# Latent attention with a gated feed-forward: one row maximum over two spans, a low half on GpSimd, and new owners for small steps

## The chip, the cores and the metric

The kernel runs on one core of a Trainium2 chip. The metric is the device time of one execution in microseconds (us). A core has five engines that run side by side, each with its own queue of instructions: TensorE (PE), VectorE (DVE), ScalarE (ACT), GpSimd (POOL) and SyncE (SP), which here issues nearly all DMAs. They wait for one another through semaphores.

## The reference, cut to what matters

`x` is 1 x 2048 x 256. After a layer norm it goes through causal attention of 16 heads with latent keys (a 64 wide latent and a 64 wide rotated part) and, beside it, through a gated feed-forward; the results are multiplied and added to `x`.

```
q = (x @ wq); kva = x @ wkv_a
ckv = rmsnorm(kva[..., :64]) * kv_norm_scale;  k_pe = rope(kva[..., 64:])
scores = (q_nope . k_nope + rope(q_pe) . k_pe) * scale, causal
out = softmax(scores) @ v @ wo
g = silu(down(silu(gate(xn)) * up(xn)));  x = x + out * g
```

## The kernel before, in words

Heads go in 8 pairs, A and B. The weights are absorbed, so that each head scores a 128 wide query against one 128 x 2048 key tile. In float32 every product is split into a high and a low half: queries and keys into `_hi` and `_lo` (three matmuls for one product), probabilities into two float16 halves.

The attention is a pipeline of 128 units `u`, 16 to a pair. Unit `u` belongs to head `u % 2` and takes two tiles of 128 query rows: a big one, tile 15 - k, and a small one, tile k, with `k = step_of(u) = u % 16 // 2` from 0 to 7. Its keys come in three spans: span 0, keys 0 to 1023 of the big tile; span 1, the rest of the big tile, (8 - k) x 128 wide; span 2, the small tile, (k + 1) x 128 wide. So spans 1 and 2 together are always 1152 wide. The text below calls `u % 16` the step, 0 to 15. What a unit passes through:

- PE: `scores` of the spans into five PSUM banks (`s_ps`). Banks of span 1 directly follow those of span 0. A bank is written again only after the exponential of the unit before has read it.
- DVE: `row_max` (L922). One maximum over span 0, one over span 1 (both to `part_max`, L929), a small one over these two (L932), and one over span 2 (L927).
- ACT: `exponentials` (L789) of each span to `prob`, `prob_high` (L795, recorded on L726) to the high half in `hl`. Its order is exp 0, exp 1, high 0, exp 2, the jobs, high 1, high 2. Exp 0 of unit u + 1 waits for the low half of span 0 of unit u, since `prob0` has one buffer.
- The low half `hl = prob - hl`: of span 0 on POOL (`("low", u)`, recorded on L1097), of spans 1 and 2 on DVE (L938).
- SP: one transposing DMA for span 0 (`turn_first`, L459), one for spans 1 and 2 (`turn_rest`, L466).
- PE: `weigh` (L637 to L639), two units later, accumulates the output in `o_ps`, in which the two tiles of one unit have two pieces of 65 columns; DVE `normalise` (L945, L950) reads them, once in each unit, and `weigh` of the next unit waits for it.

Between these stand jobs of a hand-written plan (`JOBS_OWN`, `JOBS_NEXT`, `JOBS_BEFORE`), at most two to a unit: the query projections `qA0` to `qB3` (1.4 us of PE each, in steps 0 to 3 for this pair, 8 to 11 for the next), output transposes and projections, weights. The rotary part of the queries goes in groups of 512 columns, both heads at once: ACT copies it to `q_pe` (L750), SP swaps its halves with four DMAs to `q_swap` (L453), POOL multiplies by cosine (`rope.0`) and sine (`rope.1`) and adds head A's half (`rope.2`), DVE adds head B's half to `pe_b` (L886), and POOL splits the sums (`A..hi`, `A..lo`, `B..hi`, `B..lo`). POOL has these in steps 2 to 7 and 10 to 15 (`POOL_OWN`, `POOL_NEXT`), after the low half of span 0 of the unit. `q_pe` and `q_swap` have one buffer each: ACT's copy of the next group waits for the swap of the group before (L748, L749).

POOL's instructions form one chain: each waits for the one before. After the attention comes the feed-forward in 24 slices, whose weights are loaded and prepared in the last pair.

## Time and profile before

| | |
|---|---|
| median of 3 runs | 1127.04 us (1126.23 to 1129.42) |
| the profiled execution | 1129.4 us, span 1127.6 us |
| PE busy | 975.5 us, 87% |
| DVE busy | 894.6 us, 79% |
| ACT busy | 734.8 us, 65% |
| POOL busy | 674.3 us, 60% |
| mean granted clock of PE | 0.955 |

The span runs from the first to the last instruction; the execution's own time is 1.8 us longer. Busy time is the time in which an instruction of the engine was in flight; matmuls overlap, so PE's share does not say how much more it could do. Times inside the span count from its start.

### The profile page before, as it was taken

Reading aid. Unit: us, or ns where it says so; the run is one execution under the profiler, and the core shown is the slowest. Engines: PE = TensorE matmul, PEld = TensorE weight load, DVE = VectorE, ACT = ScalarE, POOL = GpSimd, SP = SyncE. Lnnn points to the kernel's source line nnn. Section 1 sums busy time; section 2 is a strip of 40 time slices with the busy share of each in tenths; the row PEclk is TensorE's granted clock in tenths of the full one; section 3 lists DMA queues with packets and bytes.
Section 4 is the critical chain, followed back from the end, with each engine's and each line's share of the span. In section 5 each row is a group of like instructions: output and inputs, shape, how many; then the busy total and the mean of one; then the engine's idle time right before and its main releaser. Section 6 shows DMA issues by size and latency. Waiting matters only on the chain.

```text
span 1127.6 us, 26426 instructions
## 1 busy us (share of the span) xinstructions
PE 975.5 (87%) x10560; PEld 835.3 (74%) x10560; DVE 894.6 (79%) x1383; ACT 734.8 (65%) x1061; POOL 674.3 (60%) x448
## 2 busy tenths in 40 slices
PE   5658898889897989898998889898989898779998
PEld 5536777777786868776877777777778686668887
DVE  5757988897989898889888888888898889772134
ACT  1327786777667867777777777687768686662232
POOL 3655957584849484848485757666675657522332
PEclk7869999999999999999999999999999999899999
DMA  5019999999999999999999998999999899992001
GB/s 164 9 47 173 175 185 156 180 158 180 160 178 159 176 172 178 169 166 171 170 166 167 174 168 165 170 174 163 187 158 182 156 169 199 181 182 75 1 20 57
DMA packets 591979, 170.24 MB, mean 151 GB/s; under 512 B 574064, under 2 KB 585968, under 8 KB 591856
## 3 DMA queue, kind: packets, MB, share of 16 engines
q1 hardware_dynamic: 587376, 167.89, 83.5%
q8 instruction: 84, 1.38, 0.5%
q10 hardware_dynamic: 4480, 0.66, 0.4%
q14 instruction: 39, 0.32, 0.1%
HBM read 15.41 MB, written 2.10 MB: 16 GB/s over the span
## 4 chain that ended last, share of the span: by engine, by line
DVE 19%; PE 19%; issue 7%; SPq 6%; POOL 5%; ACT 3%; DMA 1%; ACTq 0%; POOLq 0%
DVE hl L938 8%; PE s_ps L523 8%; PE s_ps L621 5%; DVE part_max L929 4%; DVE neg_max L927 3%; SPq L459 2%; PE slot_ps L523 2%; SPq L466 2%; POOL hl L1097 2%; PE o_ps L523 2%; POOL pe L1097 1%; DVE acc L901 1%; SPq L453 1%; ACT hl L726 1%; DVE pe_b L886 1%
## 5 line engine op out<-in xcount | busy, mean ns | idle before, releaser
L789 ACT ACTIVATE prob<-s_ps,neg_max 128x1024 f32<-128x1024 f32 (+7 forms) x384 | 318.6, 865 | 209.1 <-DVE neg_max L927 122.2
L1097 POOL TENSOR_TENSOR hl<-prob,hl 128x1024 f16<-128x1024 f32 x128 | 288.3, 2252 | 238.1 <-ACT hl L726 235.5
L929 DVE TENSOR_REDUCE part_max<-s_ps 128x1 f32<-128x1024 f32 (+7 forms) x256 | 244.2, 984 | 80.5 <-PE s_ps L621 66.9
L726 ACT ACTIVATE hl<-prob 128x1024 f16<-128x1024 f32 (+7 forms) x384 | 296.4, 806 | 7.1 <-DMA pT<-hl 5.7
L637 PE MATMUL o_ps<-v,pT 128*128 128x65 f16 x2176 | 232.1, 194 | 65.6 <-DVE o_tiles L950 62.3
L938 DVE TENSOR_TENSOR hl<-prob,hl 128x768 f16<-128x768 f32 (+7 forms) x256 | 279.6, 1132 | 4.5 <-ACT hl L726 2.2
L637 PEld LDWEIGHTS o_ps<-v,pT 128*128 128x128 f16 x2176 | 206.5, 98 | 71.2 <-issue 67.4
L638 PE MATMUL o_ps<-v,pT 128*128 128x64 f16 x2176 | 232.6, 197 | 0.0
L639 PE MATMUL o_ps<-v,pT 128*128 128x65 f16 x2176 | 231.6, 193 | 0.0
L639 PEld LDWEIGHTS o_ps<-v,pT 128*128 128x128 f16 x2176 | 205.9, 100 | 0.0
L638 PEld LDWEIGHTS o_ps<-v,pT 128*128 128x128 f16 x2176 | 205.2, 98 | 0.0
L621 PE MATMUL s_ps<-K_hi,QA_hi 128*128 128x512 f32 (+3 forms) x320 | 126.4, 395 | 20.2 <-DVE K_lo L866 10.1
L621 PE MATMUL s_ps<-K_hi,QB_hi 128*128 128x512 f32 (+3 forms) x320 | 127.1, 397 | 18.1 <-ACT prob L789 18.0
L621 PE MATMUL s_ps<-K_hi,QB_lo 128*128 128x512 f32 (+3 forms) x320 | 120.9, 378 | 0.0
L621 PE MATMUL s_ps<-K_lo,QB_hi 128*128 128x512 f32 (+3 forms) x320 | 120.1, 375 | 0.0
L621 PE MATMUL s_ps<-K_lo,QA_hi 128*128 128x512 f32 (+3 forms) x320 | 119.3, 373 | 0.0
L621 PE MATMUL s_ps<-K_hi,QA_lo 128*128 128x512 f32 (+3 forms) x320 | 119.2, 373 | 0.0
L927 DVE TENSOR_REDUCE neg_max<-s_ps 128x1 f32<-128x256 f32 (+7 forms) x128 | 96.2, 752 | 1.9
L621 PEld LDWEIGHTS s_ps<-K_hi,QA_hi 128*128 128x128 f32 x320 | 62.2, 194 | 34.8 <-ACT prob L789 15.5
L621 PEld LDWEIGHTS s_ps<-K_hi,QB_hi 128*128 128x128 f32 x320 | 62.1, 194 | 32.9 <-ACT prob L789 23.7
L1233 POOL TENSOR_TENSOR hid_lo<-hid,hid_hi 128x512 fp32r<-128x512 f32 x24 | 31.4, 1309 | 75.1 <-ACT hid_hi L726 75.1
L621 PEld LDWEIGHTS s_ps<-K_hi,QB_lo 128*128 128x128 f32 x320 | 62.7, 196 | 10.4
(183 smaller groups left out, 1994.2 us busy)
## 6 DMA issues: line engine op xcount, KB each, us to landing
q_swap<-q_pe SPq DMA_DIRECT2D x128, 64.0 KB, 2.0
pT<-hl SPq DMA_TRANSPOSE x256, 4.8
wq_sb<-in_L_attn_wq_dram SPq DMA_DIRECT2D x8, 384.0 KB, 4.2
acc<-in_L_attn_x_dram SPq DMA_DIRECT2D x4, 512.0 KB, 6.6
wo_sb<-in_L_attn_wo_dram SPq DMA_DIRECT2D x8, 256.0 KB, 3.2
x_in<-in_L_attn_x_dram SPq DMA_DIRECT2D x1, 2048.0 KB, 8.3
out_dram<-y SPq DMA_DIRECT2D x8, 256.0 KB, 2.1
wkvs<-in_L_attn_wkv_b_dram SPq DMA_DIRECT2D x8, 128.0 KB, 4.1
```

Source lines behind the costliest of these rows:

```text
L523: last = nc.tensor.matmul(out_ap, a, b, start=(i == 0), stop=(i == n - 1))
L621: mm = nc.tensor.matmul(s_ps[:, b, 0:c], a[:, q], kk[:, k0 + c0:k0 + c0 + c], start=(j == 0), stop=(j == 2 and not ends))
L637: nc.tensor.matmul(whole, pT[:, b, :], v[:, kb, 0:LORA + 1], start=(m != 1 and b == 0), stop=False)
L638: nc.tensor.matmul(part, pT[:, b, :], v[:, kb, LORA + 1:VW], start=False, stop=False)
L639: last = nc.tensor.matmul(whole, pT[:, n + b, :], v[:, kb, 0:LORA + 1], start=False, stop=(m > 0 and b == n - 1))
L726: return nc.scalar.activation(dst, src, ACT.Copy)
L789: nc.scalar.activation(prob_of(u, m), score_bank(u, m), ACT.Exp, bias=neg_max[:, r:r + 1]).then_inc(exp_done, 1)
L927: nc.vector.tensor_reduce(neg_max[:, r:r + 1], src, AX.X, ALU.max, negate=True).then_inc(max_ready, 1)
L929: nc.vector.tensor_reduce(part_max[:, u % 2, m:m + 1], src, AX.X, ALU.max).then_inc(part_done, 1)
L938: nc.vector.tensor_tensor(both[:, w:2 * w], prob_of(u, m), both[:, 0:w], ALU.subtract).then_inc(lo_dve, 1)
L1097: return lambda: nc.gpsimd.tensor_tensor(dst, a, b, op)
L1233: nc.gpsimd.tensor_tensor(hid_lo[:, n % 2, it, :], hid[:, j % 2, :], hid_hi[:, n % 2, it, :].bitcast(F32), ALU.subtract).then_inc(hid_lo_d ...
```

## The change

- `row_max`: one maximum over spans 0 and 1 together, straight from the adjacent banks, negated; `part_max` and the small maximum go. It waits for the scores of span 1.
- VectorE's order in a unit: maximum of the big tile, maximum of the small tile (span 2, which stood last), the jobs, one low half.
- The low half of the narrower of spans 1 and 2 (`smaller(u)`: span 2 in steps 0 to 7, span 1 in steps 8 to 15; 128 to 512 wide) goes to POOL as `("rest", u)`, the last of its unit; `turn_rest` and the exponentials two units on wait for both parts.
- POOL's add of the rotary part covers both heads, and head B's half is then copied to `pe_b` by ACT (`rope_of_b`), after the jobs of steps 4, 6, 12 and 14, in place of DVE's add.
- `q_pe` and `q_swap` get two buffers each; the waits look two groups back.
- `normalise` runs once for two units; `o_ps` holds four pieces.

```
+def smaller(u):
+    return 2 if step_of(u) < HALF // 2 else 1
...
-POOL = Steps(POOL_SETUP + [name for u in range(NU) for name in [("low", u)] + steps_at(u)])
+POOL = Steps(POOL_SETUP + [name for u in range(NU) for name in [("low", u)] + steps_at(u) + [("rest", u)]])
...
-        q_pe = ab("q_pe", [P, BANK])
-        q_swap = ab("q_swap", [P, BANK])
+        q_pe = ab("q_pe", [P, 2, BANK])
+        q_swap = ab("q_swap", [P, 2, BANK])
...
             def turn_rest(u):
-                sp.wait_ge(lo_dve, 2 * u + 2)
+                sp.wait_ge(lo_dve, u + 1)
+                sp.wait_ge(pool_done, POOL.after(("rest", u)))
...
-                if m == 0 and u >= 1:
-                    pe_eng.wait_ge(norm_done, u)
+                if m == 0 and head_of(u) == 0 and u >= 2:
+                    pe_eng.wait_ge(norm_done, u // 2)
...
-                    if n >= 1:
-                        before = GROUP_ORDER[(n - 1) % NG], (n - 1) // NG
-                        act.wait_ge(swapped, 64 * n)
+                    if n >= 2:
+                        before = GROUP_ORDER[(n - 2) % NG], (n - 2) // NG
+                        act.wait_ge(swapped, 64 * (n - 1))
...
+            def rope_of_b(g, pair):
+                n = group_no(g, pair)
+                act.wait_ge(pool_done, POOL.after((f"rope{g}.2", pair)))
+                if n >= 2:
+                    before = GROUP_ORDER[(n - 2) % NG], (n - 2) // NG
+                    act.wait_ge(pool_done, POOL.after((f"B{before[0]}lo", before[1])))
+                copy(pe_b[:, n % 2, :], pe[ROPE:P, n % 2, :]).then_inc(rope_b, 1)
...
             def row_max(u, m):
-                src = score_bank(u, m)
                 r = (2 * u + m // 2) % 4
-                dve.wait_ge(scores_ready, scores_through(u, m))
-                if m == 2:
-                    nc.vector.tensor_reduce(neg_max[:, r:r + 1], src, AX.X, ALU.max, negate=True).then_inc(max_ready, 1)
-                    return
-                nc.vector.tensor_reduce(part_max[:, u % 2, m:m + 1], src, AX.X, ALU.max).then_inc(part_done, 1)
-                if m == 1:
-                    dve.wait_ge(part_done, 2 * u + 2)
-                    nc.vector.tensor_reduce(neg_max[:, r:r + 1], part_max[:, u % 2, :], AX.X, ALU.max, negate=True).then_inc(max_ready, 1)
+                src = score_bank(u, 2) if m else s_ps[:, 0:2 + len(banks(u, 1)), :].rearrange("p b c -> p (b c)")[:, 0:W0 + width(u, 1)]
+                dve.wait_ge(scores_ready, scores_through(u, m or 1))
+                nc.vector.tensor_reduce(neg_max[:, r:r + 1], src, AX.X, ALU.max, negate=True).then_inc(max_ready, 1)
...
             for u in range(-1, NU + LAG + 1):
-                if u >= LAG + 1:
+                if u >= LAG + 1 and head_of(u - LAG - 1) == 1:
                     normalise(u - LAG - 1)
                 if u + 1 < NU:
                     row_max(u + 1, 0)
-                    row_max(u + 1, 1)
+                    row_max(u + 1, 2)
                 if u <= NU:
                     for name in jobs_at(u - 1):
                         job(name)
                 if 0 <= u < NU:
-                    prob_low(u, 1)
-                    prob_low(u, 2)
-                if u + 1 < NU:
-                    row_max(u + 1, 2)
+                    prob_low(u, 3 - smaller(u))
...
-                    run((name, pair), tt(turned[0:ROPE, :], turned[0:ROPE, :], q_swap[0:ROPE, :], ALU.add))
+                    run((name, pair), tt(turned, turned, q_swap[:, n % 2, :], ALU.add))
...
             for u in range(NU):
-                prob_low(u)
+                prob_low(u, 0)
                 for name in steps_at(u):
                     step(name)
+                prob_low(u, smaller(u))
```

## Rows read from the trace of the kernel before

**Rows 1.** Stretches: us, busy (count) of PE, PEld, DVE, ACT, POOL, clock, DMA share, GB/s.

```profile
79.28:1016.00 936.72, 825.58 (x9712) 703.95 (x9712) 809.71 (x1226) 686.81 (x974) 601.89 (x365) 0.97 0.98 171
1016.00:1127.60 111.60, 106.89 (x605) 93.09 (x604) 35.43 (x47) 31.66 (x57) 31.41 (x24) 0.97 0.12 38
```

**Rows 2.** Stretches of the fourth pair (u 48 to 63), cut at exp 0.

```profile
427.26:447.09 19.83, 19.53 (x247) 17.03 (x244) 16.71 (x29) 15.88 (x22) 7.47 (x5) 1.00 0.99 185
447.09:456.65 9.56, 8.55 (x88) 7.02 (x87) 7.10 (x11) 6.37 (x10) 5.80 (x4) 1.00 0.97 164
456.65:463.05 6.40, 5.26 (x71) 4.43 (x70) 6.24 (x10) 6.25 (x9) 5.28 (x4) 1.00 0.96 178
463.05:493.07 30.02, 25.78 (x285) 22.32 (x286) 27.64 (x40) 19.58 (x31) 23.38 (x16) 0.94 0.96 160
493.07:505.83 12.76, 12.76 (x153) 11.06 (x152) 11.13 (x20) 11.64 (x16) 5.47 (x3) 1.00 1.14 194
505.83:514.61 8.78, 8.78 (x113) 7.62 (x112) 6.59 (x12) 6.36 (x9) 4.62 (x4) 1.00 1.02 160
514.61:528.09 13.48, 10.26 (x120) 8.77 (x119) 12.98 (x19) 10.36 (x15) 11.12 (x8) 1.00 0.95 164
528.09:543.72 15.63, 13.42 (x161) 10.83 (x160) 14.08 (x20) 9.52 (x14) 13.13 (x9) 0.89 0.97 165
```

**Rows 3.** Timeline of PE, steps 1 and 2: start, length, instruction.

```profile
436.03 0.39 PE L621 MATMUL s_ps<-K_hi,QA_hi 128*128 128x512 f32 x1
436.26 0.39 PE L621 MATMUL s_ps<-K_lo,QA_hi 128*128 128x512 f32 x1
...
442.20 0.40 PE L621 MATMUL s_ps<-K_hi,QB_hi 128*128 128x512 f32 x1
```

**Rows 4.** Timeline of all engines, step 3; in brackets the idle time before.

```profile
450.20 2.15 POOL L1097 TENSOR_TENSOR hl<-prob,hl 128x1024 f16<-128x1024 f32 x1 [1.82 <-ACT hl L726]
...
450.23 2.43 SPq L453 DMA_DIRECT2D q_swap<-q_pe  x4
...
454.14 0.59 ACT L726 ACTIVATE q_pe<-slot_ps 64x512 f32<-64x512 f32 x1 [3.04 <-issue]
454.20 1.28 POOL L1097 TENSOR_TENSOR q_swap<-q_swap,sinT 128x512 f32<-128x512 f32 x1 [1.86 <-DMA q_swap<-q_pe]
```

**Rows 5.** Timeline of POOL, steps 1, 5 and 6.

```profile
443.75 1.03 POOL L1097 TENSOR_TENSOR wkvs<-wkvs,scale_sb 64x512 f32<-64x512 f32 x1 [4.46 <-ACT hl L726]
...
466.63 2.32 POOL L1097 TENSOR_TENSOR hl<-prob,hl 128x1024 f16<-128x1024 f32 x1
...
473.69 2.33 POOL L1097 TENSOR_TENSOR hl<-prob,hl 128x1024 f16<-128x1024 f32 x1
```

**Rows 6.** Timeline of DVE and POOL, step 13: two low halves beside POOL.

```profile
522.61 2.27 DVE L938 TENSOR_TENSOR hl<-prob,hl 128x256 f16<-128x256 f32 x2
522.74 1.18 POOL L1097 TENSOR_TENSOR QB_hi<-pe_b,ones 64x512 fp32r<-64x512 f32 x1 [0.72 <-DVE pe_b L886]
...
524.20 2.66 POOL L1097 TENSOR_TENSOR hl<-prob,hl 128x1024 f16<-128x1024 f32 x1 [0.28 <-ACT hl L726]
```

**Rows 7.** Groups by shape, whole span: busy us, mean ns, then idle before.

```profile
L637 PE MATMUL o_ps<-v,pT 128*128 128x65 f16 x2176 | 232.1, 194 | 65.6 <-DVE o_tiles L950 62.3 <-DMA pT<-hl 3.3
...
L789 ACT ACTIVATE prob<-s_ps,neg_max 128x1024 f32<-128x1024 f32 x160 | 176.7, 1114 | 118.8 <-DVE neg_max L932 74.8 <-DVE neg_max L927 32.9 <-POOL hl L1097 10.2
L929 DVE TENSOR_REDUCE part_max<-s_ps 128x1 f32<-128x1024 f32 x144 | 175.6, 1219 | 78.2 <-PE s_ps L621 66.9 <-PE s_ps L624 11.2
...
L1097 POOL TENSOR_TENSOR q_swap<-q_swap,sinT 128x512 f32<-128x512 f32 x32 | 41.6, 1299 | 33.2 <-DMA q_swap<-q_pe 32.1
L1097 POOL TENSOR_TENSOR QB_hi<-pe_b,ones 64x512 fp32r<-64x512 f32 x32 | 41.4, 1294 | 8.9 <-DVE pe_b L886 7.2
...
L932 DVE TENSOR_REDUCE neg_max<-part_max 128x1 f32<-128x2 f32 x128 | 19.8, 155 | 4.4
...
L1097 POOL TENSOR_TENSOR wc_lo<-wq_sb,wc_hi 128x256 fp32r<-128x256 f32 x8 | 6.2, 776 | 0.6
...
L1097 POOL TENSOR_TENSOR up_raw<-up_raw,up_scale 128x1536 f32<-128x1536 f32 x2 | 5.5, 2749 | 6.0 <-DMA down_scale<-in_L_ffn_down_s_dram 6.0
```

More of the change, by code:

```diff
@@ L567, in out_job @@
                 if name.startswith("outT"):
-                    pe_eng.wait_ge(norm_done, pair * PU + 4 * q + 4)
+                    pe_eng.wait_ge(norm_done, (pair * PU + 4 * q + 4) // 2)
                     for j in range(BLK):
@@ L745, in prep_job @@
                     n = group_no(g, pair)
-                    if n >= 1:
-                        before = GROUP_ORDER[(n - 1) % NG], (n - 1) // NG
-                        act.wait_ge(swapped, 64 * n)
+                    if n >= 2:
+                        before = GROUP_ORDER[(n - 2) % NG], (n - 2) // NG
+                        act.wait_ge(swapped, 64 * (n - 1))
                         act.wait_ge(pool_done, POOL.after((f"rope{before[0]}.0", before[1])))
-                    copy(q_pe[h * ROPE:(h + 1) * ROPE, :], ps[0:ROPE, :])
+                    copy(q_pe[h * ROPE:(h + 1) * ROPE, n % 2, :], ps[0:ROPE, :])
                     if pair > 0:
@@ L780, in job @@
                     prep_job(*name)
+            def rope_of_b(g, pair):
+                n = group_no(g, pair)
+                act.wait_ge(pool_done, POOL.after((f"rope{g}.2", pair)))
+                if n >= 2:
+                    before = GROUP_ORDER[(n - 2) % NG], (n - 2) // NG
+                    act.wait_ge(pool_done, POOL.after((f"B{before[0]}lo", before[1])))
+                copy(pe_b[:, n % 2, :], pe[ROPE:P, n % 2, :]).then_inc(rope_b, 1)
             def exponentials(u, m):
@@ L786, in exponentials @@
                 elif m > 0 and u >= 2:
-                    act.wait_ge(lo_dve, 2 * (u - 2) + 2)
+                    act.wait_ge(lo_dve, u - 1)
+                    act.wait_ge(pool_done, POOL.after(("rest", u - 2)))
                 r = (2 * u + m // 2) % 4
@@ L812, in _ @@
                     prep_job(*name)
+                if name == ("qA0", 0):
+                    rope_of_b(3, 0)
+            rope_of_b(0, 0)
             for u in range(NU + 1):
@@ L821, in _ @@
                 if u < NU:
+                    pair, k = divmod(u, PU)
+                    if k in ROPE_B_OWN:
+                        rope_of_b(ROPE_B_OWN[k], pair)
+                    if k in ROPE_B_NEXT and pair < PAIRS - 1:
+                        rope_of_b(ROPE_B_NEXT[k], pair + 1)
                     prob_high(u, 1)
@@ L877, in query_lo @@
                                         ALU.subtract).then_inc(dve_freed, 1)
-            def rope_of_b(g, pair):
-                n = group_no(g, pair)
-                dve.wait_ge(pool_done, POOL.after((f"rope{g}.1", pair)))
-                if n >= 2:
-                    before = GROUP_ORDER[(n - 2) % NG], (n - 2) // NG
-                    dve.wait_ge(pool_done, POOL.after((f"B{before[0]}lo", before[1])))
-                nc.vector.tensor_tensor(pe_b[:, n % 2, :], pe[ROPE:P, n % 2, :], q_swap[ROPE:P, :], ALU.add).then_inc(rope_b, 1)
             def out_job(name, pair):
@@ L1051, in _ @@
                 if 0 <= u < NU:
-                    pair, k = divmod(u, PU)
-                    if k in ROPE_B_OWN:
-                        rope_of_b(ROPE_B_OWN[k], pair)
-                    if k in ROPE_B_NEXT and pair < PAIRS - 1:
-                        rope_of_b(ROPE_B_NEXT[k], pair + 1)
-                    prob_low(u, 1)
-                    prob_low(u, 2)
-                if u + 1 < NU:
-                    row_max(u + 1, 2)
+                    prob_low(u, 3 - smaller(u))
             def finish(u):
@@ L1119, in rope_step @@
                     done = ((queries_split, n - 1),) if 2 <= n < 4 else ()
-                    run((name, pair), tt(turned, q_pe[:], cosT[:, query_cols(g)], ALU.mult), (hi_done, after("hi", (f"qB{g}", pair))),
+                    run((name, pair), tt(turned, q_pe[:, n % 2, :], cosT[:, query_cols(g)], ALU.mult), (hi_done, after("hi", (f"qB{g}", pair))),
                         (tables_loaded[g], 32), *done)
                 elif i == 1:
-                    run((name, pair), tt(q_swap[:], q_swap[:], sinT[:, query_cols(g)], ALU.mult), (swapped, 64 * (n + 1)))
+                    run((name, pair), tt(q_swap[:, n % 2, :], q_swap[:, n % 2, :], sinT[:, query_cols(g)], ALU.mult), (swapped, 64 * (n + 1)))
                 else:
-                    run((name, pair), tt(turned[0:ROPE, :], turned[0:ROPE, :], q_swap[0:ROPE, :], ALU.add))
+                    run((name, pair), tt(turned, turned, q_swap[:, n % 2, :], ALU.add))
             def split_step(name, pair):
@@ L1160, in step, with prob_low @@
                     split_step(*name)
-            def prob_low(u):
-                both = halves_of(u, 0)
-                run(("low", u), tt(both[:, W0:2 * W0], prob0[:], both[:, 0:W0], ALU.subtract), (prob_hi, scores_through(u, 0)))
+            def prob_low(u, m):
+                w = width(u, m)
+                both = halves_of(u, m)
+                run(("rest" if m else "low", u), tt(both[:, w:2 * w], prob_of(u, m), both[:, 0:w], ALU.subtract), (prob_hi, scores_through(u, m)))
             def rotate(name, src, dst, c_buf, s_buf, n, *waits):
```

29 lines of the change are left out of this document (13 added, 16 removed).

## The prediction, made before the changed kernel ran

> **What bounds the kernel now.** I read the stretches first, then the attention pair by pair, then single steps. The attention takes 936.7 us of the span; in it PE is busy 88%, DVE 86%, ACT 73%, POOL 64% and the DMA engines 98% [rows 1]. No single engine fills it, so I cut one pair, u 48 to 63, at each unit's exp 0 on ACT (116.46 us in all, the sum of its eight rows) [rows 2]. The reader is to see two kinds of steps.
>
> Packed steps: 0 to 2 and 9 to 10. PE is busy without a gap (12.76 of 12.76 us) [rows 2]. One such step with a query projection runs from 436.03 to 442.20, 6.17 us, its matmuls of 512 columns 0.23 us apart [rows 3]. The edits take nothing from PE, so these steps can't get shorter.
>
> Heavy steps: 3 to 8 and 11 to 15, where POOL has the rotary work. They are of two kinds again. Step 3 (9.56 us) and step 11 (8.78 us) are held by the one buffer of `q_pe`: SP starts the four swaps at 450.23, they land near 454.1, and ACT, which has to copy the next group into `q_pe`, stands idle 3.04 us for it; POOL waits 1.86 us for the same landing [rows 4]. In steps 4 to 8 and 12 to 15 PE has gaps (10.26 busy of 13.48) and DVE is nearly always busy (12.98 of 13.48) [rows 2]. POOL is full there too: from its span 0 low half at 466.63 to the next at 473.69, 7.06 us, neither shows a wait before it [rows 5]. Across the run PE waits 62.3 us for `normalise`, which DVE reaches late, and exp waits for both final maxima [rows 7].
>
> DVE and POOL are not independent. In rows 6, DVE starts two low halves of 256 and 896 columns at 522.61. By the price per column below they would take some 1.4 us and take 2.27, to 524.88, that is 0.96 us after POOL's instruction ended at 523.92: the second stood until POOL was done. POOL's next one then takes 2.66 us where it takes 2.15 undisturbed [rows 4, 6], ending 1.98 us after DVE's. So each such meeting costs POOL the length of DVE's instruction less about 0.15 us. The Trainium skill, SBUF — State Buffer, section Who interferes with whom, says that a DVE instruction with two SBUF inputs and a GpSimd instruction that reads SBUF exclude one another, the second blocked until the first is done; the trace agrees. By the rule taken whole, without the 0.15 us, the ten heavy steps would cost 1.5 us more a pair.
>
> **The change part by part.**
>
> *Two buffers for the swap.* ACT's 3.04 us go, in steps 3 and 11. What is late next is POOL: the sine step waits for the landing all the same, since SP starts the swap behind the same transpose. It is not hidden, it only stops holding ACT.
>
> *Merged maximum.* A maximum of 1024 columns takes 1.219 us and the small one 0.155 [rows 7]; that is (1.219 - 0.155) / 1024 = 1.04 ns a column and 0.155 fixed. Gone are 0.155 fixed and the small maximum, 0.3 us of DVE a unit. But the first half no longer runs under the scores of span 1. The loop from scores to scores is now, in steps 0 and 1: 12 matmuls x 0.23 = 2.8, 0.2 until the last has drained, 2048 columns 2.28, exp 1.11 [rows 3, 7], 0.1 of handovers: 6.5 us against the 6.17 that PE needs. With 1920 columns in steps 2 and 3 it is 6.2, later less. So +0.3 us in two steps of a pair.
>
> *Maximum of the small tile ahead of jobs and low half.* Exp 2 stops waiting; DVE may stand up to 0.8 us for those scores. DVE has the room afterwards, so nothing on the path.
>
> *Low half to POOL.* DVE loses 128 to 512 columns, 0.3 to 0.7 us. POOL gains an instruction a unit. Its price is not in the trace at these types: 256 columns of float32 take 0.776 us, 512 take 1.299 (both with some waiting for DVE) [rows 7]; the 1024 columns of span 0 take 2.15 [rows 4], 2.1 ns each with no fixed part, so 0.54 and 1.07. I take 0.45, 0.7, 0.95 and 1.2 us for 128 to 512, near the middle. It is the last of its unit in POOL's chain, and `low` of the next unit, for which exp 0 of the unit after that one waits, queues behind it.
>
> *Head B's half to ACT.* POOL's add is not longer (it works along the 512 columns). ACT gets 0.59 us as the copy of that shape [rows 4] in four steps, hidden because POOL holds those steps.
>
> *`normalise` once for two units.* PE's 62.3 us of waits [rows 7] mostly go, but in heavy steps they are the shadow of DVE and POOL being late, so I count them inside the chain below and not on top.
>
> **The sum for this pair.** POOL's chain in heavy steps: `low` 2.15; a high half 1.03 (as the like-shaped `wkvs` [rows 5]); every other rotary step 1.28; gaps 0.07; the one DVE low half 0.6 to 0.8 (640 to 896 columns x 1.04 ns, less 0.13). `low` can start 3.1 us after exp 0 (447.09 to 450.20) [rows 2, 4], if POOL is free.
>
> - Steps 3 to 8, from exp 0 of step 3 at t = 0. The swap lands at 7.1. Sine, add, high 3.6, rest 0.7, gaps 0.4: `low` of step 4 at 11.8, done 13.95. Step 4: 1.28 + 1.28 + 1.03 + 0.95 + 0.35 + 0.7 = 5.6, `low` of 5 done at 21.7. Step 5: 3.85 + 0.95 + 0.35 + 0.7 = 5.85, done 29.7. Step 6: 1.03 + 1.28 + 0.9 + 1.2 + 0.35 + 0.6 = 5.35, done 37.2. Step 7: 5.2, done 44.55. Exp 0 of step 9 follows at 44.6; before it was 9.56 + 6.40 + 30.02 = 45.98. Gain 1.4.
> - Steps 11 to 15. `low` of step 12 again near 11.8 (the landing at about 6.3, then DVE's low half in front of the sine). Step 12: 5.45, done 21.55; step 13: 5.7, done 29.4; step 14: 3.95, done 35.5; 0.5 for the merged maximum, which now ends later: 36.0. Before: 8.78 + 13.48 + 15.63 = 37.89. Gain 1.9.
> - Steps 0 to 2, 19.83 before: `rest` of step 1 stands behind `wkvs`, which waits 4.46 us for its load [rows 5], and in front of `low` of step 2: +0.7, and 0.1 back elsewhere: 20.4. Loss 0.6.
> - Steps 9 and 10: 12.76 to 12.5. Gain 0.3.
>
> Together 116.5 to 113.5, 3.1 us a pair with the unrounded values. Seven pairs: 22 us. The last pair gains about 1.5 in its first half, and loses as much in its second: `rest` of step 6 delays SP's loads of the feed-forward weights, for which POOL already waits 6.0 us [rows 7], and `rest` of step 8 stands behind that. The setup and the 111.6 us after the attention [rows 1] are untouched. The profiled execution took 1129.4 us with 1.8 outside the span; 1129.4 - 22 = 1107.4. It was 2.4 above the median of 1127.04, so against the median: 1105.
>
> **The rivals.**
>
> *POOL has more room than I think.* The trace for it: averaged over the attention POOL is 64% busy [rows 1]. If `rest` is at its lower price and DVE's instruction falls into POOL's waits, 1.3 us less in each of 9 steps, but no shorter than ACT and PE allow: some 5 us a pair more, 40 in all: 1065. Against it: two `low` in a row without a wait [rows 5].
>
> *DVE's relief is POOL's burden.* Each `rest` at its upper price (+0.1) and each meeting at full length with a handover (+0.25), ten heavy steps: 3.5 us a pair, and nothing is left: 1127 to 1130. The Trainium skill, Perfetto Trace Analysis, section Optimizing Scalar/DVE Operations, warns that moving work between GpSimd and VectorE might not help since they share a read port. Rows 6 and the full POOL of rows 5 bear it out as a danger; the 3.04 us of the swap speak against it, as they have nothing to do with it.
>
> *Slower: the merged maximum sets the packed steps.* Its low half is last in DVE's unit; if it waits there for POOL's 2.15 us `low` [rows 4], `normalise` and the maximum behind it come late, and no part of the maximum runs ahead any more. That needs more than 1.2 us of delay: after exp 0, DVE has 0.3 small maximum, 0.7 job, 1.1 low half, 0.4 to 0.8 `normalise`, 2.9 in all, and the scores are ready after 4.2. At 1 us over in eight steps of each pair, 64 us less the 22: 1127 + 42 = 1169; at half of it 1137. Against it: POOL's `low` starts 3.1 us after exp 0, when DVE's is done. The same page's section says that breaking instructions up may let work finish sooner where an engine makes bubbles for others, which speaks against the merge; the trace shows DVE's maxima starting on PE's scores.
>
> **How the numbers follow.** My forecast 0.5 (its own range 1090 to 1118), more room 0.2, burden 0.12, slower 0.1; 0.08 for a small gain or loss elsewhere. The time is the likeliest one's, 1105. The range reaches to the other cases: down to 1075, which takes in the dearer half of the first rival, and up to 1129 for the second; outside are about 0.1 on either side. A difference under 0.3% (3.4 us) can't be told from none here. Faster 0.76, the same 0.12, slower 0.12.
>
> **What would show it.** In the trace after: no idle time of ACT before `q_pe`; steps 3 and 11 at about 7 us, steps 4 to 7 and 12 to 14 at 7.3 to 8 with POOL's `low`, rotary steps and `rest` back to back; steps 0 and 1 at 6.5 with the maximum of about 2.28 us on the path from scores to exp; DVE well under 80% busy in the attention; PE's wait for `o_tiles` near zero. POOL idle in heavy steps would make me wrong towards faster; packed steps at 7 us, or PE waiting for `pT`, towards slower.

## The result, and the profile after

The changed kernel takes 1149.41 us (median of 4 runs, 1144.36 to 1158.63), against 1127.2 for the kernel before (median of 4). The ratio is 1.0192, 95% interval 1.0141 to 1.0242: slower by 1.9%, where 1105 us were predicted. The four times go with PE's mean granted clock: 1144.36 us at 0.969, 1146.63 at 0.965, 1152.18 at 0.957, 1158.63 at 0.950. The profiled execution is the slowest of them, with a span of 1156.8 us, and stands 9 us (0.8%) above their median. Line numbers in the rows are those of each kernel's own file.

The fourth pair cut at exp 0, in the kernel after (columns as in the stretches of [rows 1]; the rows are steps 0, 1, 2, 3, 4, 5 to 8, 9 and 10, 11, 12, 13 to 15, and their sum):

```profile
438.24:446.00 7.76, 6.49 (x80) 5.72 (x80) 4.87 (x7) 4.46 (x7) 4.81 (x4) 1.00 1.00 193
446.00:453.31 7.31, 6.50 (x76) 5.66 (x77) 4.68 (x6) 5.65 (x8) 2.15 (x1) 1.00 1.12 154
453.31:459.64 6.33, 6.33 (x77) 5.32 (x76) 5.02 (x7) 5.77 (x8) 3.66 (x4) 1.00 0.86 191
459.64:466.94 7.30, 6.53 (x77) 5.47 (x75) 4.16 (x5) 6.13 (x10) 4.76 (x3) 1.00 1.02 158
466.94:475.14 8.20, 7.00 (x83) 5.84 (x79) 5.89 (x8) 7.00 (x11) 7.16 (x6) 1.00 0.88 167
475.14:504.94 29.80, 26.13 (x317) 22.57 (x317) 20.05 (x25) 20.04 (x32) 28.23 (x21) 1.00 0.90 160
504.94:517.52 12.58, 12.58 (x150) 10.88 (x151) 9.00 (x10) 11.53 (x16) 7.54 (x5) 1.00 1.10 179
517.52:525.11 7.59, 6.84 (x78) 5.62 (x76) 4.64 (x6) 6.25 (x9) 3.39 (x3) 1.00 1.09 174
525.11:534.38 9.27, 8.16 (x86) 6.91 (x86) 7.31 (x10) 6.40 (x10) 7.16 (x6) 1.00 0.99 160
534.38:557.13 22.75, 17.65 (x208) 14.47 (x208) 13.45 (x13) 14.64 (x20) 21.57 (x16) 0.92 0.91 173
sum 118.89, PE 104.21 PEld 88.45 DVE 79.08 ACT 87.86 POOL 90.44; mean PE 10.42 PEld 8.85 DVE 7.91 ACT 8.79 POOL 9.04
```

The pair takes 118.89 us where 113.5 were predicted and 116.46 stood before [rows 2]. Against the prediction: steps 0 to 2 take 21.40 us (20.4 predicted), steps 3 to 8 45.30 (44.6), steps 9 and 10 12.58 (12.5), steps 11 to 15 39.61 (36.0). Packed steps at 7 us were its own sign of being wrong towards slower, and steps 0 and 1 take 7.76 and 7.31. In steps 5 to 8 POOL is busy 28.23 of 29.80 us: there its chain is the bound, as predicted (30.65 by the prediction's own times for these four steps). The reader is to see where it is not. In steps 0 and 1 PE, DVE, ACT and POOL all have gaps: DVE is busy 4.87 of 7.76 us and yet late. Its timeline there:

```profile
435.91 2.49 DVE L940 TENSOR_REDUCE neg_max<-s_ps 128x1 f32<-128x2048 f32 x2 [3.04 <-PE s_ps L628]
438.31 0.68 DVE L888 TENSOR_TENSOR oT_lo<-slot_ps,oT_hi 128x512 fp32r<-128x512 f32 x1
...
443.67 2.49 DVE L940 TENSOR_REDUCE neg_max<-s_ps 128x1 f32<-128x2048 f32 x2 [2.86 <-PE s_ps L628]
446.08 1.28 DVE L914 TENSOR_TENSOR acc<-slot_ps,acc 128x512 f32<-128x512 f32 x2
```

and PE's:

```profile
439.14 0.36 PE L527 MATMUL slot_ps<-wvo_hi,oT_hi 128*128 128x256 f32 x1 [1.27 <-DVE oT_lo L888]
446.81 0.50 PE L527 MATMUL slot_ps<-xT_hi,wc_hi 128*128 128x512 f32 x1 [1.18 <-DVE acc L914]
```

DVE stands 3.04 us for the scores, then takes both maxima (the two are one row of 2.49 us), and only then the job whose result PE's next job needs; PE stands 1.27 us for it, and 1.18 us a step later. In the kernel before the same wait, for `oT_lo`, came to 1.4 us in the whole run. Over the whole run, the waits of PE, DVE, ACT and POOL after (total, times, longest):

```profile
DVE neg_max L940 <- PE s_ps L628: 308.8, 174, 10.7
POOL hl L1097 <- ACT hl L730: 132.4, 61, 7.7
ACT prob L803 <- POOL hl L1097: 120.5, 63, 3.2
...
POOL q_swap L1097 <- DMA q_swap<-q_pe: 47.9, 17, 4.6
...
PE slot_ps L527 <- DVE oT_lo L888: 28.3, 29, 1.3
...
ACT pe_b L730 <- POOL pe L1097: 27.6, 20, 5.9
...
PE slot_ps L527 <- DVE QB_lo L898: 17.3, 28, 1.1
...
PE slot_ps L527 <- DVE acc L914: 13.0, 14, 1.2
```

PE waits 58.6 us for DVE's jobs (28.3 + 17.3 + 13.0). ACT waits 120.5 us for POOL's low half where the same wait was 10.2 [rows 7]. That is not 110 us more of waiting: all that the exponentials wait comes to 214.1 us (120.5 and 93.6 for the maxima), where before it was 207.2 (10.2, and 197.0 for the maxima). What changed most is which wait ends last. POOL's sine waits 47.9 us for the swap where it was 32.1 [rows 7]. Of PE's 62.3 us for `normalise` [rows 7] 2.8 are left, as the change meant, and DVE's busy share of the span fell from 79 to 63%. DVE does less, and what it does stands later.

By groups: the merged maximum of 2048 columns takes what was predicted (2.28 us). The low halves on POOL take 0.54, 0.90, 0.92 and 1.18 us for 128, 256, 384 and 512 columns, where 0.45, 0.7, 0.95 and 1.2 were predicted:

```profile
L940 DVE TENSOR_REDUCE neg_max<-s_ps 128x1 f32<-128x2048 f32 x16 | 36.7, 2292 | 61.5 <-PE s_ps L628 61.5
...
L1097 POOL TENSOR_TENSOR hl<-prob,hl 128x512 f16<-128x512 f32 x32 | 37.6, 1177 | 3.9 <-ACT hl L730 1.9
...
L1097 POOL TENSOR_TENSOR hl<-prob,hl 128x256 f16<-128x256 f32 x32 | 28.8, 899 | 2.5
L1097 POOL TENSOR_TENSOR hl<-prob,hl 128x128 f16<-128x128 f32 x32 | 17.3, 540 | 3.5 <-ACT hl L730 1.2
```

The two narrowest are 20 and 28% dearer than predicted, 0.1 and 0.2 us each. That is small against the miss. What failed was where things stand.

### The profile page after: what moved, and what is told of

Read it like the earlier page. It is cut to its first block, busy times and chain, and to the rows that moved or that the text cites. A ratio compares the mean times of both kernels' runs of the same rounds, so it can differ in the third digit from the quotient of the medians.

```text
span 1156.8 us, 26105 instructions
## 1 busy us (share of the span) xinstructions
PE 987.7 (85%) x10560; PEld 841.2 (73%) x10560; DVE 724.2 (63%) x839; ACT 750.9 (65%) x1093; POOL 781.4 (68%) x576
## 4 chain that ended last, share of the span: by engine, by line
POOL 35%; PE 28%; DVE 9%; DMA 8%; SPq 6%; issue 6%; ACT 5%; ACTq 1%; POOLq 0%
POOL hl L1097 15%; PE s_ps L625 11%; PE s_ps L527 9%; POOL pe L1097 6%; DVE neg_max L940 6%; POOL q_swap L1097 4%; DMA pT<-hl 4%; PE slot_ps L527 4%; DMA q_swap<-q_pe 3%; SPq L456 3%; ACT prob L803 2%; POOL QA_hi L1097 2%; POOL QB_lo L1097 2%; POOL QA_lo L1097 2%; SPq L470 2%
## 5 line engine op out<-in xcount | busy, mean ns | idle before, releaser
L940 DVE TENSOR_REDUCE neg_max<-s_ps 128x1 f32<-128x1792 f32 (+15 forms) x256 | 324.6, 1289 | 310.6 <-PE s_ps L628 308.8
L1097 POOL TENSOR_TENSOR hl<-prob,hl 128x1024 f16<-128x1024 f32 (+4 forms) x256 | 387.1, 1512 | 147.7 <-ACT hl L730 132.4
L803 ACT ACTIVATE prob<-s_ps,neg_max 128x1024 f32<-128x1024 f32 (+7 forms) x384 | 318.5, 863 | 218.1 <-POOL hl L1097 120.5
L641 PE MATMUL o_ps<-v,pT 128*128 128x65 f16 x2176 | 229.5, 193 | 7.0 <-DMA pT<-hl 4.2
L642 PE MATMUL o_ps<-v,pT 128*128 128x64 f16 x2176 | 230.1, 196 | 0.0
L643 PE MATMUL o_ps<-v,pT 128*128 128x65 f16 x2176 | 228.9, 192 | 0.0
L946 DVE TENSOR_TENSOR hl<-prob,hl 128x1024 f16<-128x1024 f32 (+3 forms) x128 | 182.7, 1428 | 1.9
L625 PE MATMUL s_ps<-K_hi,QA_hi 128*128 128x512 f32 (+3 forms) x320 | 128.8, 402 | 32.8 <-ACT prob L803 23.6
L625 PE MATMUL s_ps<-K_hi,QB_hi 128*128 128x512 f32 (+3 forms) x320 | 126.3, 395 | 19.7 <-ACT prob L803 19.7
L1097 POOL TENSOR_TENSOR q_swap<-q_swap,sinT 128x512 f32<-128x512 f32 x32 | 52.0, 1625 | 49.1 <-DMA q_swap<-q_pe 47.9
L527 PE MATMUL slot_ps<-xT_hi,wc_hi 128*128 128x512 f32 x122 | 54.1, 443 | 35.0 <-DVE oT_lo L888 13.2
```

What stands on the lines that cost most here:

```text
L527: last = nc.tensor.matmul(out_ap, a, b, start=(i == 0), stop=(i == n - 1))
L625: mm = nc.tensor.matmul(s_ps[:, b, 0:c], a[:, q], kk[:, k0 + c0:k0 + c0 + c], start=(j == 0), stop=(j == 2 and not ends))
L641: nc.tensor.matmul(whole, pT[:, b, :], v[:, kb, 0:LORA + 1], start=(m != 1 and b == 0), stop=False)
L642: nc.tensor.matmul(part, pT[:, b, :], v[:, kb, LORA + 1:VW], start=False, stop=False)
L643: last = nc.tensor.matmul(whole, pT[:, n + b, :], v[:, kb, 0:LORA + 1], start=False, stop=(m > 0 and b == n - 1))
L803: nc.scalar.activation(prob_of(u, m), score_bank(u, m), ACT.Exp, bias=neg_max[:, r:r + 1]).then_inc(exp_done, 1)
```

## The experiments

Times are medians of 4 to 10 runs. The experiments ran in four sets (1 to 4, 5 to 8, 9 to 12, 13 to 16), beside which the kernel before took 1130.06, 1130.33, 1129.69 and 1129.86 us; ratios are to it, with the 95% interval. "Kernel 3" is the kernel of experiment 3, and so on. Three letters name the parts in dispute: **M** the merged maximum, **O** the small tile's maximum ahead of VectorE's jobs, **R** one low half on GpSimd.

**1. The changed kernel with the jobs ahead of the small maximum (M, R).**

```
-                    row_max(u + 1, 2)
                 if u <= NU:
                     for name in jobs_at(u - 1):
                         job(name)
+                if u + 1 < NU:
+                    row_max(u + 1, 2)
```

> The changed kernel, but VectorE does its jobs ahead of the small tile's maximum (big maximum, jobs, small maximum, low half). Changed kernel: 1149. Theory Jobs (TensorE's next job needs VectorE's last one, which stands behind both maxima; in steps 0 and 1 the loop is scores 2.8, drain 0.2, maximum 2.29, small maximum 0.28, job 0.68, PE job 1.5 = 7.75 us): steps 0 and 1 fall by 0.3 us each, steps with a wider small tile by up to 0.8; about 1137 to 1143. Theory Path (only the longer way scores to maximum to exp counts): jobs are not on it, 1149 within noise. Theory Pool (the added low half on GpSimd is the cost): 1149 too.

Measured: 1144.57 us, ratio 1.0135 (1.0087 to 1.0183). That is 5 us below the changed kernel and within the intervals of the two, so it can't be told from nothing; it falls between the theories (1137 to 1143, and 1149). O is not the whole of it.

**2. The changed kernel with two part maxima (O, R).** Order as changed, and in `row_max`:

```
+                for i in range(2):
+                    dve.wait_ge(scores_ready, scores_through(u, i))
+                    nc.vector.tensor_reduce(part_max[:, u % 2, i:i + 1], score_bank(u, i), AX.X, ALU.max).then_inc(part_done, 1)
```

> The changed kernel with the two part maxima of before (span 0, span 1, then the small one over both) in place of the merged one; order otherwise as changed. Theories Jobs and Path: the maximum of span 0 runs under span 1's scores again, about 1 us off the loop in steps 0 to 2, 14, 15; 1149 to about 1120, steps 0 and 1 at 6.6 us. Theory Pool: no change, 1149; steps 4 to 8 and 12 to 14 stay at 7.1 to 7.9 us under every theory.

Measured: 1135.91 us, 1.0055 (1.0031 to 1.0078). 13.5 us back, about half of what the theories Jobs and Path had (1120); the theory Pool had none.

**3. Both of these (R).**

> Both of the two runs before: two part maxima and the jobs ahead of the small tile's maximum. Jobs: best of the three, about 1110 to 1115, steps 0 and 1 at 6.2 to 6.3 us as before the change. Path: like the two maxima alone, about 1120. Pool: 1149.

Measured: 1126.5 us, 0.9977 (0.9951 to 1.0003). 23 us back, less than the theories Jobs (1110 to 1115) and Path (1120) had, and no difference from before that can be told. The three parts that no letter names and R together are worth nothing.

**4. The changed kernel with both low halves on VectorE (M, O).** `("rest", u)` leaves POOL's chain:

```
-                    prob_low(u, 3 - smaller(u))
+                    prob_low(u, 1)
+                    prob_low(u, 2)
```

> The changed kernel with both low halves of spans 1 and 2 on VectorE again (no rest on GpSimd), merged maximum and order as changed. Theory Pool: faster, GpSimd's heavy steps lose 0.7 to 1.3 us each, some 8 us a pair of which half shows, about 1120. Theories Jobs and Path: the heavy steps gain a little, but VectorE's low halves are last in its unit and push the next normalise and maximum back by 0.5 to 1.2 us wherever it has no room; 1140 to 1160.

Measured: 1153.26 us, 1.0214 (1.0175 to 1.0253). The theory Pool (1120) falls. In the presence of M and O it is of no use to free POOL. Taken alone this run would have cleared R; the later ones show that it must not be read so.

**5. The kernel before with two buffers for `q_pe` and `q_swap`, and nothing else.** The waits of the swap and of its readers look two groups back as well.

```
-        q_pe = ab("q_pe", [P, BANK])
-        q_swap = ab("q_swap", [P, BANK])
+        q_pe = ab("q_pe", [P, 2, BANK])
+        q_swap = ab("q_swap", [P, 2, BANK])
...
-                    if n >= 1:
-                        before = GROUP_ORDER[(n - 1) % NG], (n - 1) // NG
-                        act.wait_ge(swapped, 64 * n)
+                    if n >= 2:
+                        before = GROUP_ORDER[(n - 2) % NG], (n - 2) // NG
+                        act.wait_ge(swapped, 64 * (n - 1))
```

> The kernel before with the two buffers of q_pe and q_swap alone. Before: 1127 to 1130. As predicted for this part, ScalarE's idle 3 us in steps 3 and 11 goes and part of it comes back as waits of GpSimd for the swap: 2 to 3 us a pair, about 1108. Rival (the landing of the swap sets both steps anyway): no change, 1127.

Measured: 1098.37 us, 0.9724 (0.9688 to 0.976). More than was expected of it (1108). Its fourth pair takes 111.50 us, where it took 116.46 [rows 2]; its steps 3, 4, 5 to 8, and 11:

```profile
436.61:442.80 6.19, 6.19 (x77) 5.36 (x75) 6.06 (x10) 6.12 (x10) 4.16 (x2) 1.00 0.75 170
442.80:450.41 7.61, 7.41 (x88) 6.38 (x85) 7.42 (x11) 6.35 (x10) 6.37 (x5) 1.00 1.22 174
450.41:478.09 27.68, 24.75 (x288) 21.14 (x288) 27.28 (x40) 19.62 (x31) 26.13 (x16) 1.00 1.02 182
...
490.42:496.97 6.55, 6.55 (x80) 5.71 (x78) 5.28 (x10) 6.24 (x9) 2.36 (x2) 1.00 1.15 172
```

Step 3 falls from 9.56 us [rows 2] to 6.19, in which PE has no gap, and step 11 from 8.78 to 6.55. One edit of six gives more than was forecast for all.

**6. The kernel before with M alone.** `row_max` as in the changed kernel, one call less:

```
-                    row_max(u + 1, 1)
```

> The kernel before with the merged maximum alone (order: merged maximum, jobs, both low halves, small maximum). Theory Jobs: in steps 0 and 1 the loop scores 2.8, drain 0.2, maximum 2.29, VectorE job 0.68, TensorE job 1.5 gives 7.5 us against 6.7 and 6.2; VectorE, which has no room in the heavy steps, is later there too; about 1150. Theory Path (as predicted, 6.5 us): 1130 to 1135.

Measured: 1131.71 us, 1.001 (0.9986 to 1.0035). Nothing that can be told. The theory Jobs (1150) falls here; the theory Path had 1130 to 1135.

**7. The kernel before with R alone.** `turn_rest` and the exponentials two units on wait for POOL's part too, as in the changed kernel.

```
-POOL = Steps(POOL_SETUP + [name for u in range(NU) for name in [("low", u)] + steps_at(u)])
+POOL = Steps(POOL_SETUP + [name for u in range(NU) for name in [("low", u)] + steps_at(u) + [("rest", u)]])
...
-                    prob_low(u, 1)
-                    prob_low(u, 2)
+                    prob_low(u, 3 - smaller(u))
```

> The kernel before with the narrower low half on GpSimd alone. GpSimd's chain in the heavy steps as predicted (7.6, 7.7, 7.9 us in steps 4 to 6) against VectorE's relief in steps 7, 14 and 15 (8.7, 7.2, 8.4 before): about even, 1120 to 1135. If GpSimd's chain is the cost of the change: 1145 and more.

Measured: 1143.77 us, 1.0127 (1.0088 to 1.0166): 13 us lost, between what was expected (1120 to 1135) and its rival (1145 and more).

**8. Kernel 3, and SP issues the swaps ahead of the transpose of span 0.**

```
-                turn_first(u)
                 for name in jobs_at(u - 1):
                     if name[0].startswith("qB"):
                         swap(int(name[0][2:]), name[1])
+                turn_first(u)
```

> The changed kernel with two part maxima, jobs ahead of the small maximum, and SyncE issuing the swap ahead of the span 0 transpose of the same unit. Without the last part it ran 1126. Theory Landing (the swap lands 8 us after exp 0 of step 3 or 11, since SyncE issues it behind two transposes, and GpSimd's chain starts from there): it lands 2 us sooner or more, steps 3 and 4 together and 11 and 12 together fall from 15.0 and 16.5 to 13 to 14, some 4 us a pair: about 1100. Rival (GpSimd's own work sets those steps): 1126.

Measured: 1093.86 us, 0.9674 (0.9629 to 0.972). 32.6 us better than kernel 3, somewhat more than expected: with R, the landing of the swap is on the path.

**9. Kernel 5 with the swaps first**, by the diff of kernel 8.

> The kernel before with two buffers for q_pe and q_swap (that alone took 1098.4 us), and SyncE issues the four swaps ahead of the transpose of span 0 in its unit. If the landing of the swap is what holds POOL's sine, and with it the low halves of the two units that follow, this takes another 2 to 3 us from each pair: 1075 to 1085 us. If the landing is hidden once ACT no longer waits for it, the time stays within 0.5% of 1098.

Measured: 1099.68 us, 0.9723 (0.9687 to 0.976), against 1098.37. The theory falls as it stood: without R the landing is hidden.

**10. Two buffers, head B's copy on ACT, one `normalise` for two units: the change without M, O and R.** Against the kernel before, beside the diff of kernel 5:

```
-                if u >= LAG + 1:
+                if u >= LAG + 1 and head_of(u - LAG - 1) == 1:
                     normalise(u - LAG - 1)
...
-                    run((name, pair), tt(turned[0:ROPE, :], turned[0:ROPE, :], q_swap[0:ROPE, n % 2, :], ALU.add))
+                    run((name, pair), tt(turned, turned, q_swap[:, n % 2, :], ALU.add))
```

> The kernel before with three parts of the change: two buffers, head B's half copied by ACT, one normalise for two units. Left out are the merged maximum, VectorE's order and the low half on GpSimd. Theory (the low half on GpSimd is what makes the version with two maxima 28 us slower than two buffers alone): 1090 to 1100 us. Rival (ACT's copy, which waits for POOL's add, or the normalise of two units carries those 28 us): 1115 us or more.

Measured: 1071.76 us, 0.9485 (0.9447 to 0.9523), faster than the theory had it. The copy and `normalise` together are worth 26.6 us on top of the two buffers.

**11. Two buffers and R**, the diffs of kernels 5 and 7 together.

> The kernel before with two parts of the change: two buffers, and the low half of the narrower span on GpSimd as the last of its unit. Theory (that low half delays the transpose of spans 1 and 2, behind which SyncE issues the swap): 1118 to 1128 us, that is 20 to 30 more than two buffers alone, with steps 4 and 12 the longest. Rival (the low half on GpSimd costs only its own price beside POOL's steps): 1098 to 1108 us.

Measured: 1136.26 us, 1.0064 (1.0037 to 1.0091). R costs 37.9 us here, more than the theory's range, with step 12 the longest of its fourth pair (9.28 us), then step 14 (8.96) and step 4 (8.51). It takes back all that the buffers gave.

**12. The changed kernel whole, with the swaps first (M, O, R).**

> The changed kernel whole, and SyncE issues the four swaps ahead of the transpose of span 0 in its unit. Where that took 32.6 us from the version with two maxima and the jobs first, the same theory (late landing and late jobs are two costs that add) expects 1149 - 32 = 1117 us, 1110 to 1125. Rival (with the merged maximum and the jobs last VectorE is what is late everywhere, and the landing is hidden behind it): 1140 us or more.

Measured: 1120.87 us, 0.9924 (0.9892 to 0.9956): 28.5 us back, within the 1110 to 1125 that were expected. One moved DMA issue turns the changed kernel from slower to faster than before. POOL's wait for the landing, in this kernel:

```profile
POOL q_swap L1097 <- DMA q_swap<-q_pe: 9.2, 6, 3.5
```

**13. Kernel 10 with M.**

> The version of 1071.8 us (two buffers, head B's copy on ACT, one normalise for two units) with one maximum over spans 0 and 1, VectorE's order as before. Theory (the merged maximum delays exp 0 by about 1 us where PE sets the pace, and there alone): steps 0 and 1 0.9 us longer, two more steps half as much, some 3 us a pair: 1090 to 1100. Rival (with the merged maximum every job of PE waits for VectorE's job, and the merged maximum carries the 81 us): 1130 us or more.

Measured: 1098.98 us, 0.973 (0.9694 to 0.9766): M costs 27.2 us, as the theory had it.

**14. Kernel 10 with O.**

```
                     row_max(u + 1, 0)
+                    row_max(u + 1, 2)
                 if u <= NU:
                     for name in jobs_at(u - 1):
                         job(name)
                 if 0 <= u < NU:
                     prob_low(u, 1)
                     prob_low(u, 2)
-                if u + 1 < NU:
-                    row_max(u + 1, 2)
```

> The version of 1071.8 us with VectorE's order alone: maxima of the big tile, maximum of the small tile, jobs, low halves. Theory (the jobs behind the small maximum hold PE's next job; that order cost 9 us with the low half on GpSimd): 1080 to 1095. Rival (the order carries the 81 us by itself, since the low halves and normalise now come behind the scores of span 2): 1130 us or more.

Measured: 1142.25 us, 1.0081 (1.0043 to 1.0119; runs from 1131.94 to 1144.08). O costs 70.5 us, the most of all parts. The rival won. The profiled execution took 1133.26 us, so its trace shows some 9 us less than the median has.

**15. Kernel 10 with the small maximum behind the jobs and ahead of the low halves.**

> The version of 1071.8 us with the small tile's maximum behind the jobs and ahead of the low halves. It is also the version with two maxima and the jobs first, of 1126.5 us, with both low halves on VectorE. If the low half on GpSimd is what separates those two: 1072 to 1080. If the small maximum ahead of the low halves delays these (normalise and weigh stand behind them): 1085 us or more.

Measured: 1074.5 us, 0.9505 (0.9465 to 0.9545). Nothing lost. Kernel 3 is this one with R: R costs 52.0 us.

The only difference of kernels 14 and 15 is whether DVE's jobs stand behind or ahead of the small maximum; it is worth 67.8 us. Nearly all of it falls in steps 8 to 15, in which the small tile is 640 to 1024 columns wide. In the fourth pair steps 0 to 7 take 55.37 us in kernel 14 and 54.65 in kernel 15. Steps 8 to 15, kernel 15 and then kernel 14:

```profile
460.45:515.01 54.56, 49.09 (x592) 41.78 (x590) 46.47 (x66) 43.21 (x61) 40.17 (x24) 1.00 1.07 184
```

```profile
479.97:540.94 60.97, 51.58 (x611) 43.76 (x608) 51.83 (x68) 43.52 (x60) 43.63 (x25) 0.97 0.92 160
```

One of these steps, step 10, on DVE in kernel 15:

```profile
472.01 0.15 DVE L945 TENSOR_REDUCE neg_max<-part_max 128x1 f32<-128x2 f32 x1
472.19 0.69 DVE L897 TENSOR_TENSOR QA_lo<-slot_ps,QA_hi 64x512 fp32r<-64x512 f32 x1
472.92 0.96 DVE L939 TENSOR_REDUCE neg_max<-s_ps 128x1 f32<-128x768 f32 x1
473.91 1.43 DVE L951 TENSOR_TENSOR hl<-prob,hl 128x512 f16<-128x512 f32 x2
475.25 0.17 DVE L960 RECIPROCAL rinv<-o_ps 128x4 f32<-128x4 f32 x1
```

and kernel 14:

```profile
493.22 0.15 DVE L945 TENSOR_REDUCE neg_max<-part_max 128x1 f32<-128x2 f32 x1
494.03 0.96 DVE L939 TENSOR_REDUCE neg_max<-s_ps 128x1 f32<-128x768 f32 x1 [0.66 <-PE s_ps L628]
495.02 0.69 DVE L897 TENSOR_TENSOR QA_lo<-slot_ps,QA_hi 64x512 fp32r<-64x512 f32 x1
495.75 3.38 DVE L951 TENSOR_TENSOR hl<-prob,hl 128x512 f16<-128x512 f32 x2
499.16 0.18 DVE L960 RECIPROCAL rinv<-o_ps 128x4 f32<-128x4 f32 x1
```

with POOL's low half and PE's `weigh` of that step:

```profile
496.08 2.36 POOL L1103 TENSOR_TENSOR hl<-prob,hl 128x1024 f16<-128x1024 f32 x1 [3.77 <-ACT hl L730]
```

```profile
499.95 0.19 PE L641 MATMUL o_ps<-v,pT 128*128 128x65 f16 x1 [1.69 <-DVE o_tiles L965]
```

In this step one job of 0.69 us stands on the one side or the other. Where the job goes first it fills the time until span 2's scores are there. Where the maximum goes first DVE stands 0.66 us, and the low halves start 0.63 us later (2.53 us after the row of `neg_max<-part_max`, against 1.90). That is enough to meet POOL's low half, which starts at 496.08: the second of the two stands until POOL is done, 3.38 us in place of 1.43. `normalise` starts 5.94 us after that row, against 3.24, so 2.70 us later, and PE stands 1.69 us for it. The Trainium skill, SBUF — State Buffer, section Who interferes with whom, has the one engine blocked until the other is done; here too the trace agrees (3.38 against 1.43). In this step a small delay is not paid at its own price, but at that of what it runs into. Over the whole run of kernel 14:

```profile
ACT prob L802 <- DVE neg_max L945: 161.5, 86, 7.9
...
DVE neg_max L939 <- PE s_ps L628: 53.2, 69, 3.0
```

DVE stands 53.2 us ahead of the small maximum (10.7 in kernel 15), and the exponentials wait 161.5 us for the big one (54.5 in kernel 15, 49.1 in kernel 10). So DVE is late for the next unit's maximum too. How the 67.8 us divide over these ways was not tried.

**16. Kernel 10 with the swaps first.**

> The version of 1071.8 us, and SyncE issues the four swaps ahead of the transpose of span 0. Theory (only the low half on GpSimd makes the swap late; two buffers with the swap first took what two buffers alone took): within 0.5% of 1071.8. Rival (the landing holds steps 4 and 12 here too, which are 7.9 and 8.7 us long): 1055 us or less.

Measured: 1066.07 us, 0.9429 (0.9393 to 0.9465), 5.7 us (0.5%) below kernel 10: at the edge of what the theory allowed, with intervals that overlap. It has the lowest median of all versions, 5.7% below the kernel before.

## Why the prediction was wrong

The parts M, O and R, on the base of the other three (two buffers, copy on ACT, `normalise` for two units). Where O is not in, the small maximum stands behind the jobs, and in kernels 10 and 13 behind the low halves too, which is worth nothing either way (kernel 15):

| parts | us | added |
|---|---|---|
| none | 1071.8 | |
| M | 1099.0 | +27 |
| O | 1142.3 | +70 |
| R | 1126.5 | +52 on kernel 15, +55 on kernel 10 |
| M, O | 1153.3 | +82 |
| M, R | 1144.6 | +73 |
| O, R | 1135.9 | +64 |
| M, O, R (the change) | 1149.4 | +78 |

The change is a gain of 58 us (1129.7 to 1071.8) and a loss of 78. The three losses don't add: singly they come to 27, 70 and 52 us, which would make 1221 us, and together they cost 78, about what two of them cost. So no sum of single costs, however exact, would give 1149. The forecast had 22 us of gain for everything, so the miss of 44 us is what is left of two larger ones: the gain was 58, and the loss, which it had near nothing, was 78. (By its own times the pair falls by 3.0 us and not 3.1; nothing hangs on that.)

*The step that failed.* Three terms of the sum failed on the side of the losses: the order, the merged maximum and the low half on POOL. The merged maximum was put at 0.3 us in each of two steps and cost 27 us on kernel 10; the low half on POOL was priced only as a link of POOL's chain, without what it does to the swap, and cost 52 on kernel 15; both are taken up below. The dearest is the order: "DVE has the room afterwards, so nothing on the path." The small maximum ahead of the jobs was costed at nothing, with up to 0.8 us of standing. The standing is of that size on average (0.66 us in step 10; in all of kernel 14 53.2 us in 69 waits), though up to 3.0 us. Not checked was what is queued behind it: the job that PE's next job needs (36 us of PE's waits in kernel 14, 19.7 + 9.6 + 6.9 on `oT_lo`, `QB_lo` and `acc`, where kernel 10 has 1.4 on `oT_lo`), the low half, `normalise` (PE waits 44.1 us for it, where kernel 10 has 21.6), and the next big maximum (161.5 us against 49.1). That DVE is idle later in the unit does not help an instruction that is needed early in it. On kernel 10 it cost 70 us. In the changed kernel, where M and R already make others late, taking O out gives back 5 us (kernel 1) and 9 without M (kernel 2 to 3).

*The slower rival had the number, and its mechanism only in part.* A low half of DVE that waits for POOL's, with `normalise` and the maximum behind it late, 1137 to 1169 us: the changed kernel's 1149 lies there. That is partly luck, since in the changed kernel PE waits only 2.8 us for `normalise`. The rival was given 0.1, since the merged maximum alone did not seem to reach the 1.2 us from which it decides. Kernel 14 shows that way in step 10, reached by the order, which the rival did not name, and with 0.63 us of delay. In the changed kernel itself DVE has one low half less, and the waits are others: PE's 58.6 us for the jobs, ACT's 120.5 us for POOL.

*Merged maximum.* Its price was right (2.29 us); that it lies on the path was right; the size of the term was not. "+0.3 us in two steps" was reckoned against steps of 6.2 us, and they took 7.76 and 7.31. Most of that is M and not O: the same steps of the fourth pair take 7.55 and 7.12 in kernel 13 (M without O), and 6.69 and 6.24 in kernel 10. The prediction closed the loop from scores to scores by the exponential, 6.5 us. The longer way is by the job: the maximum, then DVE's job, then PE's job, which the expectation of experiment 6 put at 7.5 us. PE waits 23.5 us for `oT_lo`, `QB_lo` and `acc` in kernel 13. On kernel 10 M cost 27 us and on the kernel before nothing that can be told; that other waits covered it there is argued. The sentence of the Trainium skill against it (Perfetto Trace Analysis, section Optimizing Scalar/DVE Operations, on breaking instructions up) is borne out by kernel 13 and not by kernel 6.

*Low half on POOL.* R cost 52 us on kernel 15. The chain of steps 5 to 8 was right within 3% (29.80 us, 30.65 predicted). Not priced was its effect on steps 3, 4, 11 and 12: `turn_rest` waits for it, SP's next transposes and the swap stand behind that, and the swap lands later. In the changed kernel, on SP and POOL around exp 0 of step 3 (459.64):

```profile
456.86 2.65 POOL L1097 TENSOR_TENSOR hl<-prob,hl 128x128 f16<-128x128 f32 x2
457.36 2.69 SPq L470 DMA_TRANSPOSE pT<-hl  x1
...
460.14 3.37 SPq L462 DMA_TRANSPOSE pT<-hl  x1
...
462.74 2.15 POOL L1097 TENSOR_TENSOR hl<-prob,hl 128x1024 f16<-128x1024 f32 x1 [0.41 <-ACT hl L730]
463.61 2.44 SPq L456 DMA_DIRECT2D q_swap<-q_pe  x4
467.58 1.28 POOL L1097 TENSOR_TENSOR q_swap<-q_swap,sinT 128x512 f32<-128x512 f32 x1 [2.69 <-DMA q_swap<-q_pe]
468.94 2.01 POOL L1097 TENSOR_TENSOR pe<-pe,q_swap 128x512 f32<-128x512 f32 x1
```

The first row holds `rest` of step 1 and `low` of step 2. The transpose of spans 1 and 2 starts at 457.36, once `rest` is done. `low` is done at 459.51, but SP issues the earlier transpose until 460.05, so the next one starts at 460.14 and the swap at 463.61, 3.97 us after exp 0 where it was 3.14 [rows 2, 4]. The sine starts 7.94 us after exp 0, not 7.1, and POOL stands 2.69 us for it, not 1.86 [rows 4]; the add takes 2.01 us, beside a low half of DVE (1.09 us from 468.72). Steps 3 and 4 take 15.50 us where the prediction had 13.95 (`low` of step 4 done). The prediction said that SP starts the swap behind the same transpose, and then did not ask whether that transpose would come later. Kernels 8 and 12 show its worth with R, 32.6 and 28.5 us; without R it is worth -1.3 and 5.7 us (kernels 9, 16), though POOL's wait for the landing goes there too (46.1 us in kernel 10, 8.9 in kernel 16). The rival "DVE's relief is POOL's burden" had R's sign, and its 3.5 us a pair are about half of the 6.5 to 6.8 that R costs alone (52 to 55 us over eight pairs, kernel 15 or 10 to 3). A part of R's cost may come by PE's clock, which no experiment holds apart: over the first seven pairs the mean granted clock is 0.97 in kernel 3 and 1.00 in kernel 15, and PE is busy 727.13 us against 706.48 with the same 8399 matmuls, up to 20.7 of the 48.0 us between the two there. In the fourth pair of kernel 3 the clock falls in steps 7 and 14 (means of 0.76 and 0.78, a part of each at 1.2 GHz in place of 2.4), behind steps in which PE has gaps (6.43 us busy of 7.88 in step 6, 5.41 of 7.52 in step 13). With the swaps first (kernel 8) it is 1.00 again.

*Two buffers.* The mechanism was right: of ACT's idle time before `q_pe` (47.5 us over the run before) 7.2 us are left, all of it waiting for PE's matmuls, none for the swap. The term was far too small: costed as part of a chain that gains 1.4 and 1.9 us a pair together with the rest of the change, the buffers alone give 32 us, 4 a pair. POOL's chain in steps 4 to 8, which was taken to hold them up, has room for it as long as R is not in it.

*`normalise` and the copy.* "Inside the chain, not on top", no gain of their own: they give 26.6 us together. Which of the two is more was not tried.

*Setup, last pair and tail.* Exp 0 of the first unit is at 82.73 us, not 79.28 [rows 1]. Among the kernels tried it lies between 76.49 (kernel 14) and 82.85 (kernel 12), so that these 3.5 us are the change's own is not shown. The copy to `pe_b`, now on ACT, waits 27.6 us for POOL over the run, 5.9 us at most. Of the 29.2 us between the two spans the first seven pairs have 14.8 (829.80 us against 815.00), the setup 3.5, the last pair, which was forecast to come out even, 7.9 up to exp 0 of its last unit, and what follows 3.0. The cause of these last two was not tried.

*Left open.* Why all three parts together stop at 1149 is argued (each makes another engine late for the same step) and not shown. How much of R's cost is the later swap, POOL's longer chain and PE's clock is not shown either; that the swap's place is worth 32.6 and 28.5 us with R is. A step's room was never measured by itself.
